# Stacks of 96 rows with zero rows, and another order of the first loads, in a recurrent-attention and mixture-of-experts layer

## What is computed

```python
tf   = sigmoid(sum(cond))                             # one number per batch
d    = exp(-exp(w)) * (0.5 + 0.5 * tf)                # one decay per channel
nf, df = scan forward  of exp(f)*f and exp(f)         # a = a*d + input, 256 steps
nb, db = scan backward of the same
hid1 = sigmoid(x) * (nf+nb-ekv+euk*f) / (df+db-ek+euk) * (0.8 + 0.2*tf)
q, k, v = hid1 @ Wqkv.T + bqkv                        # 16 heads of 16 channels
x1   = x + softmax(q @ k.T * 4) @ v @ Wproj.T + bproj
hid2 = the same recurrence with x1 in place of x and other w, u
x2   = x1 + mixture_of_experts(hid2)                  # 64 experts, 6 of them per token, and one shared
```

## Time and profile before

| | |
|---|---|
| median of 3 runs | 422.79 us (420.14 to 424.99) |
| the profiled execution, its own time | 424.84 us |
| its span, first to last instruction | 423.0 us |
| mean granted TensorE clock over the span | 0.850 of full |
| busy: PE, DVE, ACT, POOL | 81%, 76%, 48%, 31% of the span |

### The profile page before, as it was taken

One profiled execution on the slowest core, in us unless ns is written; L12 is line 12 of the kernel. 1 busy time (PEld: TensorE's weight loads), 2 busy tenths in 40 slices (PEclk: granted clock), 3 DMA queues, 4 the chain that ended last, 5 costly groups with the idle time before them and its releaser, 6 DMA issues.

```text
span 423.0 us, 6020 instructions
## 1 busy us (share of the span) xinstructions
PE 342.7 (81%) x1552; PEld 255.9 (61%) x1552; DVE 323.0 (76%) x622; ACT 201.6 (48%) x373; POOL 129.4 (31%) x117
## 2 busy tenths in 40 slices
PE   0071369788786897996897997999999999999994
PEld 0050246456554575584575665888888788888883
DVE  4979987985988476546556899588888888888884
ACT  3212125324642165327446555466666666666661
POOL 1527453307240001002032234133333333333330
PEclk9995559658955796558589999899999999999999
DMA  6049708803470158300333455355556556556541
GB/s 203 1 57 146 131 2 98 104 3 51 75 77 2 33 69 102 101 2 8 109 97 125 127 167 172 121 188 194 192 193 184 183 196 189 193 195 182 186 158 50
DMA packets 34582, 49.32 MB, mean 117 GB/s; under 512 B 5186, under 2 KB 16386, under 8 KB 34562
## 3 DMA queue, kind: packets, MB, share of 16 engines
q1 hardware_dynamic: 34274, 48.94, 46.2%
q10 hardware_dynamic: 288, 0.14, 0.2%
HBM read 39.16 MB, written 1.33 MB: 96 GB/s over the span
## 4 chain that ended last, share of the span: by engine, by line
PE 58%; DVE 26%; issue 6%; ACT 5%; POOL 2%; DMA 1%; DVEq 0%; ACTq 0%; POOLq 0%
PE ps L1255 6%; PE ps L1257 6%; DVE scan L728 6%; PE ps L1256 6%; PE ps L1266 6%; PE ps L1267 6%; PE ps L1268 6%; PE ps L1169 4%; DVE mx L793 4%; PE ps L1126 4%; PE ps L1137 4%; PE ps L1156 3%; DVE q_st L946 2%; DVE scan L1050 2%; PE ps L1200 2%
## 5 line engine op out<-in xcount | busy, mean ns | idle before, releaser
L442 POOL TENSOR_TENSOR scan<-scan 128x512 f32<-128x512 f32 x68 | 73.1, 1075 | 142.1 <-ACT scan L572 140.4
L1055 DVE TENSOR_TENSOR qk_lo<-scan,qk_hi 128x512 fp32r<-128x512 f32 x68 | 69.2, 1018 | 31.9 <-ACT qk_hi L579 31.9
L572 ACT ACTIVATE scan<-ps 128x512 f32<-128x512 f32 x68 | 40.7, 598 | 52.4 <-PE ps L1257 52.2
L1137 PE MATMUL ps<-k_st,q_st 64*128 64x256 f32 x128 | 38.2, 419 | 26.0 <-DVE mx L793 16.0
L1266 PE MATMUL ps<-qk_hi,k_st 128*128 128x512 f32 x136 | 54.4, 400 | 4.5 <-DVE qk_lo L1055 4.3
L509 ACT ACTIVATE prob<-ps 128x512 f32<-128x512 f32 x64 | 37.0, 593 | 44.2 <-PE ps L1156 44.1
L1255 PE MATMUL ps<-hid_hi,k_st 128*128 128x512 f32 x136 | 55.1, 405 | 2.0 <-DVE q_st L946 2.0
L1257 PE MATMUL ps<-hid_hi,q_st 128*128 128x512 f32 x136 | 54.7, 402 | 0.0
L565 ACT ACTIVATE k_st<-clip 128x512 fp32r<-128x512 f32 x68 | 42.8, 631 | 24.5 <-PE ps L1268 24.5
L1256 PE MATMUL ps<-hid_lo,k_st 128*128 128x512 f32 x136 | 54.4, 400 | 0.0
L1267 PE MATMUL ps<-qk_lo,k_st 128*128 128x512 f32 x136 | 53.5, 393 | 0.0
(11 more groups left out here) (116 smaller groups left out, 467.6 us busy)
## 6 DMA issues: line engine op xcount, KB each, us to landing
clip<-in_tiles SPq DMA_DIRECT2D x68, 256.0 KB, 3.0
ex<-gates SPq DMA_DIRECT2D x136, 128.0 KB, 2.9
q_st<-qk_hi SPq DMA_DIRECT2D x16, 128.0 KB, 3.9
q_st<-qk_lo SPq DMA_DIRECT2D x16, 128.0 KB, 4.8
k_st<-qk_hi SPq DMA_DIRECT2D x16, 128.0 KB, 5.5
k_st<-qk_lo SPq DMA_DIRECT2D x16, 128.0 KB, 6.2
f_sb<-in_fT SPq DMA_DIRECT2D x4, 256.0 KB, 6.7
x_sb<-in_xT SPq DMA_DIRECT2D x4, 256.0 KB, 8.4
```

What stands on the lines that cost most here:

```text
L442: g.tensor_tensor(sq[:, k], relu[:, k], relu[:, k], ALU.mult).then_inc(sq_ready, 1)
L1055: TT(act_lo[:, k], act[:, k], act_hi[:, k].bitcast(F32), ALU.subtract).then_inc(act_lo_ready, 1)
L1137: last = mm(bank_s(n)[:, qt], q_st[0:MAXROW, slot(b, h // HB), h % HB, qt * P:(qt + 1) * P], k_st[0:MAXROW, slot(b, h // HB), h % HB, :], ...
```

## The change

It has three parts. MAXROW goes from 64 to 96: rows 64 to 95 of both stacks are zero in every slot, and the rows of maxima and ones move to 96 and 97. So the scores are 96 rows deep and the shifted scores 98. A tile `zeros` (32 x 256) is set by DVE, and two DMAs spread it over the 24 head places of `q_st` and `k_st`. Both memsets count in `ones_ready`, and PE waits for three DMAs in place of one. Second, `vec` and `cond_sb` are no longer loaded by ACT but are the first two loads of SyncE. Third, f and x of batch 2 are issued behind the second stack of batch 0 in place of between the two.

```diff
@@ constants
-MAXROW = STACK
+MAXROW = 96
@@ tiles
         ones = sb("ones", [2 * SHARED * B, S])
+        zeros = sb("zeros", [MAXROW - STACK, S])
@@ SyncE
+            sp.dma_start(vec[:], vecs).then_inc(ld_vec, 16)
+            sp.dma_start(cond_sb[:], cond.partition_broadcast(P)).then_inc(ld_vec, 16)
             load_f(0)
             load_x(0)
             sp.dma_start(wi[:], w_in).then_inc(ld_w, 16)
             load_f(1)
             load_x(1)
             sp.dma_start(bvb[:], bv.partition_broadcast(P)).then_inc(ld_w, 16)
-            sp.wait_ge(ones_ready, 1)
-            sp.dma_start(k_st[MAXROW:MAXROW + 2].rearrange("p n h s -> p (n h) s").bitcast(F32),
-                         ones[0:2].unsqueeze(1).broadcast_to([2, SLOTS * HB, S])).then_inc(ld_ones, 16)
+            sp.wait_ge(ones_ready, 2)
+            for st, r0, r1, src in ((q_st, STACK, MAXROW, zeros), (k_st, STACK, MAXROW, zeros), (k_st, MAXROW, MAXROW + 2, ones)):
+                sp.dma_start(st[r0:r1].rearrange("p n h s -> p (n h) s").bitcast(F32),
+                             src[0:r1 - r0].unsqueeze(1).broadcast_to([r1 - r0, SLOTS * HB, S])).then_inc(ld_ones, 16)
...
             load_stack(0, 0)
+            load_stack(0, 1)
             load_f(2)
             load_x(2)
-            load_stack(0, 1)
@@ ScalarE
-            sc.dma_start(vec[:], vecs).then_inc(ld_vec, 16)
-            sc.dma_start(cond_sb[:], cond.partition_broadcast(P)).then_inc(ld_vec, 16)
@@ VectorE
             v.memset(ones[:], 1.0).then_inc(ones_ready, 1)
+            v.memset(zeros[:], 0.0).then_inc(ones_ready, 1)
@@ TensorE
-            pe.wait_ge(ld_ones, 16)
+            pe.wait_ge(ld_ones, 48)
```

## The result

The changed kernel took 406.62 us (median of 4 runs, 404.61 to 408.19), the kernel before, run beside it, 422.77 (4 runs, 420.14 to 424.99): a ratio of 0.9618, interval 0.9544 to 0.9691. Run once more on another occasion it took 407.82 against 425.16, ratio 0.9653 (0.9565 to 0.9741). So it is 15 to 17 us faster. The forecast was 412.5, with a range of 405 to 422: the sign and the range held, the size was 5.9 us short, and, as the experiments show, the larger part of the gain has a cause that the prediction had put at zero. A ratio leaves out a kernel's slower executions (over 1.5% above its fastest), so it can differ from the quotient of the two medians by up to 1%.

What follows compares the result with a forecast made beforehand. PE, busy 81% and 58% of the chain, was taken to set the time where on the chain, its speed following the granted clock. Clock 8.8 plus head 1.4 saved 10.2 us from the median 422.79: 412.5, range 405 to 422.

Steps and rivals of the forecast that it cites:

- The clock: Attention part: deeper matmuls (64 to 96, 66 to 98 rows) are granted the upper clock more; 8.8 us, between 0 and 15.
- rival one: Rows don't count for the clock, only the earlier vec and cond_sb loads gain: 421.4 us; chance 0.24.
- Direct cost 0: Score and shifted-score matmuls: more rows alone don't make a matmul slower, as 64 and 66 rows cost the same; 0 us.
- PE worked without a gap: In 166.4:169.8 PE was busy 3.40 of 3.40 us on 64- and 66-row matmuls, yet the clock fell straight behind.
- 169.8 to 190.6: Batch 3's score work and output projection, PE-bound: a held clock saves 6 us, from about 3 to 7.5.
- 90 to 98: Value and score work on PE: an earlier clock rise saves one value group, 0.8 us; the projection behind gives nothing.
- 115 to 142: Stretch mostly carried by DVE; last 6 us are value groups and a projection: 1.3 us saved.
- 197 to 214: PE busy 15.76 of 17.00 us; the clock's fall stays because of waits before it, a somewhat earlier rise saves 0.7 us.
- The head: Kernel start: vec and cond_sb loaded first let the setup end at 6.2; 1.4 us saved, bounds 0.8 and 2.1.
- The zero rows at nothing, the order at nothing: Zero fill ends near 24 us, within the stack's 7 us slack; batch 2's later loads are covered: 0 each.
- Rival two: Clock granted more, but in DVE's stretches where it doesn't pay, and lost again at 169.8: 417.3 us; chance 0.18.
- Rival three: The zero fill's two DMAs into 32 partitions run slowly and delay the first stacks: up to 431 us; chance 0.05.

Runs made afterwards that it cites:

- The probe: Changed kernel plus, behind all its work, 250 matmuls at each of seven depths (64 to 128 rows); at the lower clock 0.215 us each for 66 and 80 rows.
- The head alone: Kernel before with only the vec and cond_sb loads moved to the front of SyncE's queue: 423.50 us, ratio 1.0038.
- the unread fill: Changed kernel with matmuls 64 and 66 rows deep as before; the 32 zero rows are filled behind them and never read: 422.03 us, ratio 0.9934.

## Why the prediction was right, and where it was not

*The clock.* This part of the mechanism was right. The prediction read, from 98.1:101.5 against 166.4:169.8, that the rows of a matmul count in what is granted. The probe shows it directly. It called this an inference and gave rival one, that rows don't count, a chance of 0.24. The head alone, which is all that this rival leaves, gave a ratio of 1.00. The probe excludes its reason, few columns behind each weight load: all its streams have 256, and 96 rows hold the clock.

*The step that failed: "Direct cost 0".* It said that 64 and 66 rows cost the same, 0.22 and 0.25 us each at full clock. So they do there, because both carry the switch. It took the projection as the yardstick for the cost of rows, whose operands are plain fp32, where the stacks are fp32r. The yardstick that fits lies in the same trace, the expert part, with fp32r operands, 128 rows and 512 columns. In the kernel before, PE's timeline has there, at the clock of 1.00:

```profile
299.86 0.39 PE L1266 MATMUL ps<-qk_hi,k_st 128*128 128x512 f32 x1
300.08 0.39 PE L1267 MATMUL ps<-qk_lo,k_st 128*128 128x512 f32 x1
300.31 0.39 PE L1268 MATMUL ps<-qk_hi,q_st 128*128 128x512 f32 x1
```

0.22 to 0.23 us from start to start, for twice the columns of a score that took 0.22. So a score cost nearly twice what its columns did, and the two rows told it before any run. The term was given no room below zero cost; the switch that it missed is worth about 9 of the 16 us. That the result lies inside the range is in part luck: the lower end, 405, stood for a clock held in more places and not for cheaper matmuls.

*"PE worked without a gap" was half an illusion.* In 166.4:169.8 PE is recorded busy for 3.40 of 3.40 us, but the record of a matmul includes what the switch costs. The reading "gapless and yet the clock falls" was right in its result, and weaker as evidence than it seemed: a score took 0.22 us there, and the same columns take 0.12 at this clock without a switch. The kernels with 66 and 80 rows and the probe, all without a switch, separate the two.

*169.8 to 190.6: 6 forecast, 9.6 measured*, beyond the 7.5 that was written down for a clock held throughout. It took both effects. From batch 3's first maximum to the end of the output projection it is 29.8 us before, 24.1 with 66 rows and 20.2 with 96: 5.7 by the two rows (4.6 if reckoned from the unread fill, 28.7 us) and 3.9 more by the depth. Up to the first probabilities the two rows save 3.7 without any change of the mean clock (23.04 to 19.37, clock 0.57 in both), and the depth 3.6 to 3.8 more (to 15.81 and 15.53). The step that priced the difference by pairs of rows at either level (1.15 against 0.67) compared kernels with the switch on both sides; the chain of the changed kernel has

```profile
164.84 0.57 PE ps L1140 x4
...
165.65 1.00 PE ps L1172 x16
...
173.76 1.73 PE ps L1203 x8
```

four scores in 0.57 us where the prediction put 0.67, since their switch is gone, and 1.00 and 1.73 where it put 1.07 and 1.97.

*90 to 98 (0.8 forecast) gave nothing*, -0.2 over batch 1. The way to the projection behind it did get shorter, by 1.5 us, but then the clock, which had risen at 92, fell once more:

```profile
98.90:102.30 3.40, 3.40 (x10) 2.68 (x9) 1.59 (x3) 0.60 (x1) 2.59 (x3) 0.50 0.76 78
```

In this stretch lies the projection (eight matmuls of L1129). It took 3.39 us on the chain, where before it took 1.74 at full clock; in the kernel with 66 rows it took 3.33. In the stretch ahead of this fall, 92.0 to 98.9, PE was busy for 4.46 of 6.90 us. *115 to 142 (1.3) gave 2.9* up to batch 3's first maximum. *197 to 214 (0.7) gave 2.3* from the end of the output projection to the first expert matmul. The prediction took the waits for ACT there as unmended. They stand, and the clock still falls, but for 6.8 us (180.8 to 187.6) in place of 17.0 (197.1 to 214.1). This term is the least sure: in the changed kernel's second trace the same way took 18.75 us in place of 17.40, so that 1.0 to 2.3 are saved. Another 1.75 came behind that, as the expert part's first units no longer start at the lower clock; it was not in the sum.

*The head: 1.4 forecast, 1.96 measured* at the first maximum. x_sb, which I thought would become the late one, was there. The condition landed at 4.25, where about 4.2 was taken, and the setup was over at 6.25, where 6.2 was. In the changed kernel's second trace the first maximum came at 43.04, exactly 1.4 earlier than before.

*The zero rows at nothing, the order at nothing:* right ("the fill without its use"). The fill ended near 21, forecast 24.

*Rival two* (the clock granted where it doesn't pay) has its piece in batch 1, where it rose earlier and was lost on the projection. *Rival three* needed a fill that the rate of the stack loads didn't suggest; it came true with 62 partitions, by another mechanism than the one written down.

So the medians' gain of 16.2 us, against 10.3 forecast, is made of a term that was missing, the switch (about 9, 422.03 to 412.97), and of a clock's part that, with the switch gone, came to some 5 to 7 us (412.97 to 407.82, 406.62 and 406.13) where 8.8 were forecast. The miss of 5.9 is what is left of two errors with opposite signs, the larger of them the missing switch. The medians come from several occasions, so each share is sure to 2 us or so.

## What to carry to other kernels

Matmuls of 64 rows and of more, interleaved on one PE queue, cost about 0.3 us (lower clock) or 0.19 us (upper) at each change here: pad the shallow ones past 64 rows; two zero rows sufficed. Where PE works mostly on shallow matmuls and the clock won't hold, try 96 rows; zeros did, and depth cost no time by itself. Fill pad rows by a DMA over a number of partitions that 16 divides (32 and 48 did well here, 62 did not), and before trusting "busy" of PE, divide the time between two matmuls' starts by the columns and compare it with another line of the same number format at the same clock.

## What the runs showed of the hardware that I had not expected

- 250 matmuls of 64, 66 or 80 rows, back to back for 55 us, never left the granted clock of 0.50; 96 to 128 rows were granted 1.00 and kept it.
- A pair of 256-column matmuls behind a change between 64 rows and 66 (or 98) took 0.72 us at the lower clock, against 0.43 with both above 64; at the upper 0.43 against 0.24. In the probe the single change from 64 to 66 rows cost 0.29 us at the lower clock, and those from 66 to 80 and from 80 to 96 nothing.
- The clock can be lost behind a faster stretch: in the changed kernel it fell for 98.9 to 102.3 and gave back there what the earlier rise had won.
- A fill of 3 MB over 62 partitions moved at 34 GB/s and held SyncE's next two issues for 45 us each; 1.6 MB over 32 partitions shared 172 GB/s with other loads.
- Open: why 80 rows, which the probe shows no better than 66 for the clock, had a median 2.8 us lower and a mean clock 0.01 higher than 66 on another occasion (the ratios are nearly equal); where between 80 and 96 rows the clock turns; and what PE does in the 0.2 to 0.3 us of a change.
